# A gated cross-attention and sparse feed-forward kernel: idle transposes at its start, and four rearranging copies moved from ScalarE to GpSimd

## The reference

```python
x = x + tanh(g_xattn[0]) * xattn(layernorm(x), ctx, mask)   # scores, masked softmax, readout
x = x + tanh(g_ffn[0])   * ffn(layernorm(x), w_gate, w_up, w_down)
# ffn: h = silu(x @ w_gate) * (x @ w_up)        512 -> 2048
#      of every 4 neighbours of h the 2 largest in magnitude are kept, the others are 0
#      h @ w_down                               2048 -> 512
```

## Time and profile before

| | us |
|---|---|
| median of 3 runs | 1083.94 |
| lowest and highest | 1083.72, 1084.35 |
| the profiled execution | 1086.38 |
| its span (first to last instruction) | 1084.6 |
| TensorE busy | 1070.9 |
| VectorE, ScalarE, GpSimd busy | 794.3, 614.3, 226.1 |

### The profile page before, as it was taken

The page is one execution under the profiler, slowest core; times in us unless marked ns, Lnnn a source line. Parts: engine busy times, 40 slices in busy tenths (PEclk is TensorE's granted clock), DMA queues, the critical chain, the costliest instruction groups (busy, mean ns, idle before and its releaser), DMA issues.

```text
span 1084.6 us, 15165 instructions
## 1 busy us (share of the span) xinstructions
PE 1070.9 (99%) x4972; PEld 879.4 (81%) x4972; DVE 794.3 (73%) x1389; ACT 614.3 (57%) x1126; POOL 226.1 (21%) x343
## 2 busy tenths in 40 slices
PE   7999999999999999999999999999999999999998
PEld 6888777888888888878888888878888888888887
DVE  6999879998987676676857576676856464665756
ACT  6999776777755454444544454444544444443452
POOL 7887302222111111100011111110000111111021
PEclk9999999999999999999999999999999999999999
DMA  8999985999989777787899767787798666767727
GB/s 301 323 309 323 350 355 134 329 317 289 289 268 362 174 192 189 175 271 204 241 289 285 185 177 192 180 256 203 237 306 247 153 153 155 192 151 190 199 28 144
DMA packets 89821, 252.65 MB, mean 233 GB/s; under 512 B 9104, under 2 KB 9872, under 8 KB 85648
## 3 DMA queue, kind: packets, MB, share of 16 engines
q1 hardware_dynamic: 68144, 203.45, 53.3%
q0 software_dynamic: 21600, 48.24, 26.1%
HBM read 153.09 MB, written 98.57 MB: 232 GB/s over the span
## 4 chain that ended last, share of the span: by engine, by line
PE 88%; DMA 4%; DVE 3%; ACT 2%; issue 1%; SPq 1%; POOL 0%; DVEq 0%; ACTq 0%; POOLq 0%
PE ps_y L1399 10%; PE ps_y L1401 10%; PE ps_y L1400 10%; PE ps_a L1326 9%; PE ps_a L1330 9%; PE ps_a L1328 9%; PE ps_d L1326 5%; PE ps_d L1330 5%; PE ps_d L1328 5%; PE ps_c L1353 3%; PE ps_y L1367 2%; PE ps_c L1330 2%; PE ps_c L1326 2%; PE ps_c L1328 2%; DMA x_blk<-xnT_scratch 2%; PE ps_a L1345 1%
## 5 line engine op out<-in xcount | busy, mean ns | idle before, releaser
L633 POOL DMA_DIRECT2D out_rows<-y_out x124 | 105.7, 856 | 707.5 <-ACT y_out L785 703.9
L1326 PE MATMUL ps_a<-xm,w_ring 128*128 128x512 f32 x512 | 200.2, 391 | 2.5 <-ACT cp L668 1.5
L1328 PE MATMUL ps_a<-xm,w_ring 128*128 128x512 f32 x512 | 199.6, 390 | 0.0
L1330 PE MATMUL ps_a<-xm,w_ring 128*128 128x512 f32 x512 | 199.5, 390 | 0.0
L785 ACT ACTIVATE y_out<-ps_y,ffn_gate 128x512 f32<-128x512 f32 x124 | 85.1, 688 | 182.7 <-PE ps_y L1401 182.7
L1399 PE MATMUL ps_y<-dn,h_hi 128*128 128x512 f32 x480 | 188.1, 392 | 0.3 <-ACT y_out L785 0.2
L1401 PE MATMUL ps_y<-dn,h_lo 128*128 128x512 f32 x480 | 187.2, 390 | 0.0
L1400 PE MATMUL ps_y<-dn,h_hi 128*128 128x512 f32 x480 | 186.7, 389 | 0.0
L762 ACT ACTIVATE h_hi<-hidden 128x512 fp32r<-128x512 f32 x128 | 73.2, 625 | 82.7 <-DVE hidden L1095 82.6
L1069 DVE TENSOR_TENSOR beats<-h_abs 128x512 bf16<-128x512 f32 x186 | 117.7, 684 | 1.3 <-ACT h_abs L755 1.3
L1326 PEld LDWEIGHTS ps_a<-xm,w_ring 128*128 128x128 f32 x512 | 96.1, 188 | 24.8 <-issue 3.0
(11 more groups left out here) (122 smaller groups left out, 1872.4 us busy)
## 6 DMA issues: line engine op xcount, KB each, us to landing
w_ring<-w_scratch SPq DMA_DIRECT2D x147, 512.0 KB, 4.3
out_rows<-y_out POOLq DMA_DIRECT2D x124, 256.0 KB, 4.2
w_scratch<-w_ring SPq DMA_DIRECT2D x56, 512.0 KB, 5.9
xm_scratch<-x_out SPq DMA_DIRECT2D x40, 512.0 KB, 5.5
xm<-xm_scratch SPq DMA_DIRECT2D x19, 1024.0 KB, 7.4
w_raw<-in_L_ffn_w_down SPq DMA_DIRECT2D x9, 1024.0 KB, 7.8
x_in<-in_x SPq DMA_DIRECT2D x32, 256.0 KB, 5.2
ctx_in<-in_ctx SPq DMA_DIRECT2D x32, 256.0 KB, 5.4
```

Source lines behind the costliest of these rows:

```text
L633: nc.gpsimd.dma_start(out[RING * (n // (2 * TILES * QS)) + TILES * ORDER[order] + n % TILES], y_out[:, n % 4], accum_op=ALU.add).then_inc( ...
L1326: nc.tensor.matmul(to, w_ring[:, k, e, 0, c], xm[:, k, 0, c], start=begins and c == 0, stop=False, skip_group_check=not begins)
L1328: nc.tensor.matmul(to, w_ring[:, k, e, 0, c], xm[:, k, 1, c], start=False, stop=False, skip_group_check=not begins)
L1330: last = nc.tensor.matmul(to, w_ring[:, k, e, 1, c], xm[:, k, 0, c], start=False, stop=c == 1, skip_group_check=not begins)
```

## The change

It has four groups of edits.

1. At the start TensorE makes 12, 10 and 6 transposes of the identity into a PSUM bank that nobody reads (`idle_turns`), before the first ctx transposes, before the first xn transposes and after the first scores. The order of the first three slots on TensorE is written out: scores(0) now come before x(1), and scores(1) before x(2).
2. The gates are loaded as one row by two transfers on ScalarE's queue and spread over the partitions by a matmul with a row of ones; before, SyncE loaded them as a broadcast between the input loads. The mask has a place of its own in the x operands of product 6, and its last quarter is loaded and converted later.
3. The parts i = 3 to 6 of pair 0's x, some pieces and some spreads move by one slot; both low parts of part 6 are made by VectorE in stage 0. SyncE issues piece (2,1) and load_x_blk(1, 0) after the last xnT store.
4. The four spreads of unit 2 go from ScalarE to GpSimd, around the loads after the slots. ScalarE and VectorE orders change: copy_a1(1) before dn_high(0), copy_d0 before x_high in the first half of stages from 2 on and in the second half of stage 1, gated0(0,0) earlier; x_low_at(s, 0) after add_c22 in all stages from 2.

```diff
-CONVERT = {1: 0, 3: 1, 4: 2, 7: 3}
+CONVERT = {1: 0, 3: 1, 4: 2, 21: 3}
-PIECE_AT = {6: (0, 2), 7: (0, 3), 11: (1, 0), 12: (1, 1), 28: (1, 2), 29: (1, 3), 36: (2, 0), 37: (2, 1)}
-SPREAD_AT = {5: ((0, 0),), 6: ((0, 1),), 10: ((0, 2),), 11: ((0, 3),), 21: ((1, 0),), 22: ((1, 1),)}
+PIECE_AT = {6: (0, 2), 8: (0, 3), 12: (1, 0), 13: (1, 1), 28: (1, 2), 30: (1, 3), 36: (2, 0)}
+SPREAD_AT = {5: ((0, 0),), 7: ((0, 1),), 10: ((0, 2),), 11: ((0, 3),), 22: ((1, 0),), 29: ((1, 1),)}
-         | {29 + 2 * (i - 3) + k: (k, i) for i in range(3, 7) for k in range(2)})
+         | {30 + 2 * (i - 3) + k: (k, i) for i in range(3, 7) for k in range(2)})
+IDLE_TURNS = (12, 10, 6)
...
@@ sync, after the slots
-                if n == SLOTS - 3:
-                    load_x_blk(sp, 1, 0)
+            load_w_piece(sp, nc.sync, 2, 1)
+            load_x_blk(sp, 1, 0)
@@ gpsimd, after the slots
+            spread_by_pool(2, 0)
             load_w_piece(pool, nc.gpsimd, 2, 2)
+            spread_by_pool(2, 1)
             for k in range(4):
                 pool.wait_ge(x1_stored[k], 16 * (B // 4))
...
             load_dn(0)
             load_w_piece(pool, nc.gpsimd, 2, 3)
+            spread_by_pool(2, 2)
             load_w_piece(pool, nc.gpsimd, 3, 0)
+            spread_by_pool(2, 3)
             load_w_piece(pool, nc.gpsimd, 3, 1)
@@ scalar
+            for n, g in enumerate((g_xattn, g_ffn)):
+                nc.scalar.dma_start(gates_in[:, n:n + 1], g.rearrange("(a n) -> a n", a=1)).then_inc(gates_loaded, 16)
...
-                        x_high_at(s, 0)
                         copy_d0(u, 0)
                         copy_d0(u, 1)
+                        x_high_at(s, 0)
...
-                    spread(act, 2, 0)
...
-                    spread(act, 2, 1)
...
-                    spread(act, 2, 2)
...
-                    dn_high(0, 0)
-                    dn_high(0, 1)
                     copy_a1(1, 0)
                     copy_a1(1, 1)
-                    dn_high(0, 2)
-                    dn_high(0, 3)
-                    x_high_at(0, 1)
-                    spread(act, 2, 3)
+                    for j in range(GROUP):
+                        dn_high(0, j)
                     copy_d0(1, 0)
                     copy_d0(1, 1)
+                    x_high_at(0, 1)
...
+                if s == 1:
+                    copy_d0(u, 0)
+                    copy_d0(u, 1)
                 if building:
                     spread(act, u + 1, 1)
@@ vector
-                    if s > QS:
-                        x_low_at(s, 0)
                     add_c22(u, 0)
                     add_c22(u, 1)
                     if s <= QS:
                         dn_low(dve, nc.vector, s - 1)
-                        x_low_at(s, 0)
+                    x_low_at(s, 0)
...
                     add_c11(0, 0)
                     add_c11(0, 1)
+                    dve.wait_ge(x_lo_done, 12)
+                    x_low(dve, nc.vector, 0, 0, 6)
+                    x_low(dve, nc.vector, 0, 1, 6)
...
                     add_c12(0, 0)
+                    gated0(0, 0)
                     add_c12(0, 1)
+                    gated0(0, 1)
                     w_low(dve, nc.vector, 1, 5)
-                    gated0(0, 0)
-                    gated0(0, 1)
@@ tensor
+            def idle_turns(count):
+                for i in range(count):
+                    nc.tensor.transpose(ps_av[0][:, 0:P], ident[:], ident[:])
+
+            idle_turns(IDLE_TURNS[0])
+            turn_ctx(0)
+            idle_turns(IDLE_TURNS[1])
+            turn_x(0)
+            turn_ctx(1)
+            score(0)
+            idle_turns(IDLE_TURNS[2])
+            turn_x(1)
+            turn_ctx(2)
+            score(1)
+            turn_x(2)
+
+            pe.wait_ge(ones_set, 1)
+            pe.wait_ge(gates_loaded, 32)
+            nc.tensor.matmul(ps_av[1][:, 0:2], ones[:], gates_in[:], start=True, stop=True).then_inc(gates_spread, 1)
```

More of the change, by code:

```diff
@@ L197, in flamingo_gated @@
         xattn_gate = sb("xattn_gate", [P, 1], F32, 4)
-        gates_in = sb("gates_in", [P, 2], F32, 4)
+        gates_in = sb("gates_in", [1, 2], F32, 4)
+        ones = sb("ones", [1, P], F32, 4)
         ident = sb("ident", [P, P], F32, 4)
         x_blk1 = sb("x_blk1", [P, 4, HALF], F32, 4)
-        mask_in = x1nT[:, 0, 0:2].rearrange("p c n -> p (c n)").bitcast(U8)
+        mask_in = Place((PROD - 1) * 4 * 4 * HALF)("mask_in", [P, B * M], U8, 1)
         GROUP_M = RING * M
@@ L479, in _ @@
                     load_mask(0)
-                if b == 4:
-                    for n, g in enumerate((g_xattn, g_ffn)):
-                        sp.dma_start(gates_in[:, n:n + 1], g.rearrange("(a n) -> a n", a=1)
-                                     .to_broadcast([P, 1])).then_inc(gates_loaded, 16)
                 if b in (4, 5):
@@ L569, in _ @@
             nc.gpsimd.memset(stats[:], 1.0).then_inc(stats_set, 1)
+            nc.gpsimd.memset(ones[:], 1.0).then_inc(ones_set, 1)
             nc.gpsimd.memset(least[:, 0:2], EPS)
@@ L722, in _ @@
                 if n in X0_AT:
+                    if X0_AT[n] == (0, 6):
+                        act.wait_ge(mask_neg_done, B // RING)
                     x_high(act, 0, *X0_AT[n])
@@ L938, in _ @@
                 x_high_at(s, 2)
-                copy_d0(u, 0)
-                copy_d0(u, 1)
+                if s > 1:
+                    copy_d0(u, 0)
+                    copy_d0(u, 1)
                 if building:
@@ L996, in _ @@
                         x_sum(dve, 0, *X0_AT[n])
-                if n == SLOTS - 2:
-                    dve.wait_ge(x_lo_done, 13)
-                    x_low(dve, nc.vector, 0, *X0_AT[n - 1])
                 b = n - 3
@@ L1332, in product @@
                 last.then_inc(made[k], 1)
-            for n in range(SLOTS):
-                b = n - 1
-                if 0 <= b < B:
-                    pe.wait_ge(ctx_in_loaded[b % INPUTS], 16 * (b // INPUTS + 1))
-                    wait(pe, cT_copied, b)
-                    for c in range(KC):
-                        last = nc.tensor.transpose(ps_cT[:, c], ctx_in[:, b % INPUTS, c * P:(c + 1) * P], ident[:])
-                    last.then_inc(cT_done, 1)
-                    pe.wait_ge(xn_done, b + 1)
-                    wait(pe, xT_copied, b)
-                    for c in range(KC):
-                        last = nc.tensor.transpose(ps_xT[:, c], xn[:, b % 2, c * P:(c + 1) * P], ident[:])
-                    last.then_inc(xT_done, 1)
-                b = n - 2
-                if 0 <= b < B:
-                    pe.wait_ge(xT_copied, b + 1)
-                    pe.wait_ge(cT_copied, b + 1)
-                    wait(pe, neg_scores_done, b - 1)
-                    for c in range(KC):
-                        last = nc.tensor.matmul(ps_sc[b % 2][:, 0:M], xnT[:, b % 2, c], ctxT[:, b % 2, c],
-                                                start=(c == 0), stop=(c == KC - 1))
-                    last.then_inc(scores_done, 1)
@@ new lines, in turn_ctx, with turn_x @@
+            def turn_ctx(b):
+                pe.wait_ge(ctx_in_loaded[b % INPUTS], 16 * (b // INPUTS + 1))
+                wait(pe, cT_copied, b)
+                for c in range(KC):
+                    last = nc.tensor.transpose(ps_cT[:, c], ctx_in[:, b % INPUTS, c * P:(c + 1) * P], ident[:])
+                last.then_inc(cT_done, 1)
+            def turn_x(b):
+                pe.wait_ge(xn_done, b + 1)
+                wait(pe, xT_copied, b)
+                for c in range(KC):
+                    last = nc.tensor.transpose(ps_xT[:, c], xn[:, b % 2, c * P:(c + 1) * P], ident[:])
+                last.then_inc(xT_done, 1)
@@ new lines, in score @@
+            def score(b):
+                pe.wait_ge(xT_copied, b + 1)
+                pe.wait_ge(cT_copied, b + 1)
+                wait(pe, neg_scores_done, b - 1)
+                for c in range(KC):
+                    last = nc.tensor.matmul(ps_sc[b % 2][:, 0:M], xnT[:, b % 2, c], ctxT[:, b % 2, c],
+                                            start=(c == 0), stop=(c == KC - 1))
+                last.then_inc(scores_done, 1)
+            def idle_turns(count):
+                for i in range(count):
+                    nc.tensor.transpose(ps_av[0][:, 0:P], ident[:], ident[:])
@@ L1356, in _ @@
+            for n in range(3, SLOTS):
+                if 3 < n <= B:
+                    turn_ctx(n - 1)
+                    turn_x(n - 1)
+                if 3 < n < B + 2:
+                    score(n - 2)
                 b = n - 7
```

21 lines of the change are left out of this document (12 added, 9 removed).

## The result

The change makes the kernel **slower by 0.53%**: 1090.53 us (median of 6 runs, 1088.76 to 1093.07) against 1084.58 (6 runs, 1083.72 to 1085.79), ratio 1.0053 with a 95% interval of 1.0042 to 1.0065.

A forecast was written before the change was run, and what follows sets the result against it. TensorE, busy 1070.9 of 1084.6 us, was taken to bound the kernel. Gains of 1.45 + 0.5 + 0.5 + 0.3 = 2.75 us, taken from the median 1083.94, gave 1081.2 us, range 1079.1 to 1084.6.

The forecast's parts named there:

- Reading of the kernel before and the places of loss: TensorE, idle only 13.7 us: losses at the head, around units 0 and 1, and at 200, 470 and 711 us.
- Head: First 15 us: idle transposes raise TensorE's clock near 7 us, so probs(0) starts at 13.15 instead of 14.55, 1.4 us won.
- third rival: Head: idle transposes don't raise the clock and only take time, head loses about 2 us; result 1084.6 us, chance 0.15.
- Product (2,0): Unit 0, slot 36: product waits for the part GpSimd now makes one slot later, a new stall of 0.8 us.
- End of unit 0: gated0(0,0) moves ahead, h0 comes 0.6 to 1.2 us earlier, and the 0.65 us stall before 132.93 goes.
- Unit 1: Up to unit 2's start: w_down's transfer becomes last, unit 2 starts at 153.6; 1.45 us remain won (2.9 to -0.7).
- the term for `w_down`: Unit 1: load issued at 134.4, 0.8 us earlier, landing at 142.9; net 5.5 us later add_c22(1,0) starts at 148.4.
- The sentence that gave contention no price: Unit 1: GpSimd's copies beside VectorE's instructions cost nothing, as six earlier copies took 1.13 us beside a busy VectorE.
- The bound of 0.5 for one instruction: Unit 1: at worst each GpSimd copy holds up one VectorE instruction by 0.5 us, two in the chain (1 us).
- Rival 1: Unit 1: w_down load later, as copy (2,1) needs its piece; unit 2 about 1.1 to 2 us later; 1082.7, chance 0.15.
- Stage 1: Second half: copy_d0(3) goes ahead of a 1.03 us copy and x_high, so the stall before 200.06 goes: 0.5 us won.
- From stage 2 on: copy_d0 ahead of x_high, which waits for x_blk: 0.5 us won near 470 and 0.3 us at 711.89.

The follow-up runs named there:

- stage 1's order back: The changed kernel with copy_d0 behind copy (4,1) and x_high again in the second half of stage 1: 1089.54 us, ratio 1.0044.
- late orders back: The changed kernel with x_high before copy_d0 and x_low before add_c22 again in stages from 2 on: 1087.27 us, ratio 1.0021.
- late orders alone: The kernel before with only copy_d0 before x_high and x_low after add_c22 in stages from 2 on: 1087.12 us, ratio 1.0026.

## Why the prediction was wrong

**Reading of the kernel before and the places of loss.** Right: the stalls before 132.93, 145.55 and 200.06 went, those at 470 and 711 too.

**Head, -1.4 us.** It was 1.05 at the scores of batch 2, with the first probabilities at 13.49 instead of 13.15. What was late next was named rightly, the statistics of batch 4 ahead of the scores on VectorE, but their rows came at 11.96 and not at 11.48, so the maximum was ready at 13.46 where 12.9 was expected. The rise was put near 7 and came near 5.8, so the third rival (turns that don't raise the level) is false: it was given 0.15. By the Trainium skill ("TensorE: Matmul & The Clock Gate", Part 4) transposes shouldn't bring the upper level; the rows of 5.19 and 6.85 above speak against it, four transposes in 0.66 us with only transposes before them. But the prediction gave the gain to the turns, and the run without them has all but 0.1 us of it.

**Product (2,0), +0.8.** It was 0.75 and the restart, as predicted; behind it 0.95 of the head's 1.05 us are gone.

**End of unit 0.** Right, and worth nothing, since the landing of `w_down` sets unit 2.

**Unit 1, -1.45 against +1.12 measured (-0.04 to +1.19 in the five traces with this code): the first failed step.** That the transfer of `w_down` becomes the last thing was right, and so was the 5.23 us from add_c22 to unit 2. What failed is the term for `w_down` (issue, transfer, landing to add_c22): add_c22 was put at 148.4 and came at 150.97. Three sizes were off. (1) The issue: 134.4 predicted, 135.15 measured, as the copy started at 133.78 instead of 133.15 (gated0(0,1) ended at 133.05, not 132.5, and w_low(1,5), the reader that the copy waits for, at 133.65) and took 1.43 instead of 1.13. (2) The transfer: it was taken at 8.5 us as in the earlier trace rows and took 9.9. This is the largest part, 1.4, and its cause is open. In the four traces with SyncE's old order the transfer takes 8.47 to 8.54 us, in the five with the new order and an issue near 135 it takes 9.9, 9.9, 9.9, 9.5 and 8.6. That points to the changed queues, but not by x_blk and piece (2,1) being under way with it: in the changed kernel these have landed at 132.92 and 129.64, before the load is issued. And the 8.6 stands in a kernel with the same code there. No run changed SyncE's order alone. (3) From landing to add_c22: 5.5 predicted (its terms add up to 5.6), 5.92 measured from the start of dn_high, and this with 0.9 for a GpSimd copy in it; without, it would be 5.0. The sentence that gave contention no price failed here. It rested on six copies beside which VectorE ran batch statistics, which read one tile; gated1 and dn_low read two tiles of SBUF each, and beside a copy they took 2.19 for 1.28 and 3.41 for 2.49, 0.9 each. The bound of 0.5 for one instruction was too low as well. The Trainium skill ("SBUF — State Buffer", the summary rules for kernel authors) says that a VectorE operation with two SBUF inputs and a GpSimd operation that reads SBUF block each other for the whole instruction; by that rule the price is up to one copy, 1.1 us, for each such meeting, and these rows agree with it. It should have been a rival.

Rival 1 (the load becomes later) had a chance of 0.15 and 1.5 us, and it came nearest to what happened in unit 1: the load landed 1.3 us later than in the kernel before. But that is by its transfer, as the issue is not later (135.15 against 135.21), and what held the issue was another thing than the one named: the copy waited for the reader of its block, not for its piece. Piece (2,1) was issued at 122.79 and landed at 129.64, long before the copy. More to the point is what the prediction compared: it asked whether the issue would come earlier than 135.21. It didn't ask when GpSimd *could* issue the load. With the copy out of the way this is 130.65, since piece (2,1) and x_blk now stand behind the last xnT store on SyncE, and the store lands at 127.7 instead of 134.59. The change had bought 4.5 us of lead for the load and spent it on its own copy.

**Stage 1, -0.5.** The stall went, and in the changed kernel's trace another of 1.22 us came at 213.08. It is in four traces of ten. A ScalarE copy that waited for a piece of weights stands before it, at 210.31 in the changed kernel and at 209.31 in the run with stage 1's order back, which has no stall; what decides when the piece comes is open.

**From stage 2 on, -0.8 against +1.7 in the trace, and +2.6 to +3.3 in the runs: the second failed step, and the larger one.** The stalls for copy_d0 at 470 and 711 went as predicted. But that step prices ScalarE's edit alone, in stages 6 and 10. VectorE's edit of the same stages, x_low_at behind add_c22, has no term in it: it was put at nothing without a reason. Stages 7 and 11 aren't looked at, for either edit. There x_low and x_sum had stood in VectorE's idle time before add_c22; behind it they add 1.2 us to a chain at whose end, the y_out copy, TensorE had next to no slack: 1.09 of the 1.2 us arrive. In stages 6 and 10 it is x_low alone, 0.6 us, and the stalls near 482 and 723 that were 0.33 and 0.29 become 0.60 each. That the chain from add_c22 to y_out was nearly the last thing stood in the trace, in the 0.33 us lost near 482; VectorE's timeline in stage 7 would have shown the rest, and wasn't read. How the loss divides between the two edits is not shown: they were always moved together, and in stage 7 ScalarE's alone takes x_low out of the idle time as well.

**The sum.** By the traces: +1.1 at unit 2 where -1.45 stood, +0.7 for stages 1 and 2 where -0.5 stood, +1.7 for the rest where -0.8 stood: 3.5 of the measured 3.9, the remainder being below 0.2 at any one place. By the medians the two groups cost 2.8 (copies) and 3.3 (orders) out of 5.9 us. No rival has either group cost over 2 us, and the chance of slower, 0.05, took in little more than the head.

## What to carry to other kernels

When a copy goes to an engine that also issues transfers, look at what it waits for and what is queued behind it: here a 1.1 us copy, waiting for its buffer, held a load back by 4.5 us, and placing it one line later won 2.3 us. An operation that is moved "only behind" another has a price where it leaves idle time: read, in every stage that the edit touches, what the engine waited for just before its old place. Repeat the check for each repetition of a loop, since 0.3 to 0.8 us at six places was more than all that the change won.

## What the runs showed of the hardware

Transposes alone raise TensorE's level: ten took 1.51 us where twelve before them took 2.82. A wait of 1.94 us was followed by a fall: the engine started again at 147.86 with a granted clock of 1.00 to 149.0, then matmuls stood 0.43 us apart to 152.5 (granted clock 0.51 from 149.0 to 152.1), the 1.2 GHz level, against 0.23 at 2.4 GHz. Ten matmuls in the wait removed it. The same fall came behind waits of 2.00 us (late orders back), 1.93 (stage 1's order back) and 2.27 (late orders alone). The windows of the kernel after (us; busy time and count of TensorE, its weight loads, VectorE, ScalarE, GpSimd; granted clock, DMA share, GB/s) show 0.88 and 0.95:

```profile
140.00:150.00 10.00, 8.06 (x35) 6.33 (x34) 4.69 (x7) 4.44 (x9) 2.25 (x2) 0.95 1.01 401
150.00:160.00 10.00, 8.96 (x35) 6.94 (x34) 9.86 (x17) 4.98 (x9) 0.00 (x0) 0.88 0.79 293
```

In the kernel before, the wait of 1.47 us at 145.55 left no such rows, nor did the one of 1.70 in its second trace. A GpSimd copy of 128x512 floats took 1.11 to 1.14 us beside VectorE's statistics (one SBUF input) or its additions with one input in PSUM, and in the changed kernel 1.43 and 1.53 beside gated1 and dn_low with two SBUF inputs, which lose 0.9 us to it. And a load issued 4.5 us earlier into filled queues landed only 2.1 us earlier (12.3 us instead of 9.9).
